# A decoder layer in which cross attention is one accumulating product of probabilities with context values already multiplied by the output weights

## The reference

```python
x = _layernorm(x + _L0_attn_ref(x, w_qkv, b_qkv, w_proj, b_proj))    # causal self attention, 16 heads of 16
x = _layernorm(x + _L0_xattn_ref(x, ctx, ctx, w_q, w_k, w_v, w_o))   # 16 heads of 64, 77 keys
x = _layernorm(x + _L0_ffn_ref(x, k0, k1, k2, s0, s1, s2))           # 256 -> 1024 -> 1024 -> 256, weights +1 / -1

def _L0_xattn_ref(query, key, value, w_q, w_k, w_v, w_o):
    q = (query @ w_q).reshape(B, Q, HEADS, HEAD_DIM).transpose(0, 2, 1, 3)
    k = (key @ w_k).reshape(B, Kl, HEADS, HEAD_DIM).transpose(0, 2, 1, 3)
    v = (value @ w_v).reshape(B, Kl, HEADS, HEAD_DIM).transpose(0, 2, 1, 3)
    scores = jnp.einsum('bhqd,bhkd->bhqk', q, k) * scale
    attn = jax.nn.softmax(scores, axis=-1)
    out = jnp.einsum('bhqk,bhkd->bhqd', attn, v)
    out = out.transpose(0, 2, 1, 3).reshape(B, Q, HEADS * HEAD_DIM)
    return out @ w_o
```

## Time and profile before

| what | value |
|---|---|
| time of three runs | 2335.62 us median (2334.43 to 2338.11) |
| the profiled execution: its own time | 2333.06 us |
| its span, first to last instruction | 2331.3 us |
| busy share of the span | PE 96%, PEld 79%, DVE 64%, ACT 42%, POOL 21% |
| first phase, from PE's first transpose to the last keys | 13.2 to 139.2 us |
| mean granted clock of TensorE | 0.987 |
| bytes moved by DMA | 135.85 MB |

### The profile page before, as it was taken

One profiled execution on the slowest core, in us unless ns is written; L12 is line 12 of the kernel. 1 busy time (PEld: TensorE's weight loads), 2 busy tenths in 40 slices (PEclk: granted clock), 3 DMA queues, 4 the chain that ended last, 5 costly groups with the idle time before them and its releaser, 6 DMA issues.

```text
span 2331.3 us, 52778 instructions
## 1 busy us (share of the span) xinstructions
PE 2233.6 (96%) x18516; PEld 1847.7 (79%) x18516; DVE 1485.0 (64%) x4685; ACT 970.2 (42%) x1797; POOL 482.0 (21%) x751
## 2 busy tenths in 40 slices
PE   7967899999999999999999999999999999999997
PEld 6856787888888888788888888888888888888876
DVE  3435666667667666667676666676676666676763
ACT  3313444444444444444444444444444444444432
POOL 2001212222222122212222222222221222122220
PEclk9978999999999999999999999999999999999999
DMA  6753332132333331233333322323333212233300
GB/s 209 228 115 53 54 58 45 39 50 37 56 56 56 56 50 41 42 44 49 56 56 56 56 42 39 47 41 56 56 56 56 48 40 44 40 53 56 56 25 10
DMA packets 150504, 135.85 MB, mean 58 GB/s; under 512 B 47746, under 2 KB 141986, under 8 KB 150402
## 3 DMA queue, kind: packets, MB, share of 16 engines
q1 hardware_dynamic: 150468, 135.37, 31.3%
HBM read 39.10 MB, written 28.59 MB: 29 GB/s over the span
## 4 chain that ended last, share of the span: by engine, by line
PE 81%; DVE 10%; issue 4%; ACT 3%; DMA 2%; POOL 1%; SPq 0%; DVEq 0%; POOLq 0%
PE ps L1028 10%; PE ps L1029 9%; PE ps L1169 9%; PE ps L988 8%; PE ps L1155 6%; PE ps L1011 5%; PE ps L1141 4%; PE ps L1082 4%; PE ps L1069 4%; PE ps L997 4%; DVE max L736 3%; PE ps L1039 3%; PE ps L1040 2%; PE ps L970 2%; PE ps L977 2%
## 5 line engine op out<-in xcount | busy, mean ns | idle before, releaser
L1028 PE MATMUL ps<-r_h,w 128*128 128x256 f16 x2048 | 464.4, 274 | 1.9 <-DVE r_l L682 1.9
L1029 PE MATMUL ps<-r_l,w 128*128 128x256 f16 x2048 | 462.1, 273 | 0.0
L471 ACT ACTIVATE r_h<-ps 128x512 f16<-128x512 f32 x256 | 152.6, 596 | 524.1 <-PE ps L1029 516.4
L697 DVE CUSTOM_DVE_ANT_0 junk<-ps,causal 128x128 bf16<-128x128 f32 (+1 forms) x1024 | 316.2, 353 | 60.1 <-PE ps L1058 53.8
L419 POOL TENSOR_TENSOR p<-p,inv 128x308 f32<-128x308 f32 x256 | 179.0, 699 | 479.5 <-DVE inv L753 479.5
L682 DVE SCALAR_TENSOR_TENSOR r_l<-ps,r_h 128x512 f16<-128x512 f32 x256 | 176.1, 688 | 119.5 <-ACT r_h L471 119.5
L524 ACT ACTIVATE probs<-ps 128x768 f32<-128x768 f32 x256 | 206.9, 809 | 106.9 <-PE ps L1069 106.8
L412 POOL TENSOR_SCALAR_AFFINE_SELECT probs<-probs 128x512 f32<-128x512 f32 x256 | 163.3, 638 | 393.8 <-ACT probs L524 393.7
L1028 PEld LDWEIGHTS ps<-r_h,w 128*128 128x128 f16 x2048 | 200.1, 98 | 49.6 <-issue 23.5
L1029 PEld LDWEIGHTS ps<-r_l,w 128*128 128x128 f16 x2048 | 200.9, 98 | 20.7
L758 DVE TENSOR_TENSOR o_l<-ps,o_h 128x512 fp32r<-128x512 f32 x128 | 88.5, 691 | 191.0 <-ACT o_h L516 190.6
(11 more groups left out here) (140 smaller groups left out, 4729.3 us busy)
## 6 DMA issues: line engine op xcount, KB each, us to landing
q_st<-o_h SPq DMA_DIRECT2D x192, 128.0 KB
k_bd<-o_h SPq DMA_DIRECT2D x192, 128.0 KB, 6.7
q<-q SPq DMA_DIRECT2D x128, 128.0 KB, 2.1
v_scratch<-v_out SPq DMA_DIRECT2D x44, 224.0 KB, 2.3
k_bd<-k_scratch SPq DMA_DIRECT2D x64, 154.0 KB
v<-v_scratch SPq DMA_DIRECT2D x32, 308.0 KB
x_in<-in_x SPq DMA_DIRECT2D x32, 256.0 KB, 4.6
out<-y SPq DMA_DIRECT2D x32, 256.0 KB, 2.2
```

The costliest lines, as they stand in the source:

```text
L697: dve.tensor_tensor_reduce(out=junk[:, e, b * P:b * P + width], in0=ps[:, bank + b, e * width:(e + 1) * width], in1=causal[:, (1 - b) * P: ...
L1028: pe.matmul(dst, w1[:, kk, m * P:(m + 1) * P], r0_h[:, kk, :], start=kk == 0, stop=False)
L1029: last = pe.matmul(dst, w1[:, kk, m * P:(m + 1) * P], r0_l[:, kk, :], start=False, stop=kk == KF - 1)
```

## The change

The values of a head are multiplied with that head's rows of `w_o` already in the first phase: per group and pair `context_values` makes the values transposed (heads' dimension on the partitions), ACT and DVE split them (`values_high`, `values_low`), `value_outputs` multiplies each half of 64 partitions with the 64 rows of `w_o` of its head, and the result, 256 numbers for each token and head, goes to `vo_scratch` (two halves of eight heads). In the loop a batch's 2 x 616 rows (77 tokens times 8 heads) are loaded (`load_value_outputs`), split by ACT and POOL, and used as the moving operand of `cross_output`: one product that accumulates over all token and head rows in ten tiles of 128 or 104 rows. The probabilities are laid out with eight heads innermost (`p2[P, 2, 2, 77, 8]`), transposed in those ten tiles, and split in high and low parts by ACT and DVE. `cross_values` and `cross_projection` are gone. Pieces of layer 1, self scores and self maxima are put at other places, the bank of the self scores is 2 for all pairs but 3 and 5, and self maxima 6 and 7 are made at the start of the next turn of the loop.

```diff
-            pe.wait_ge(const_pool, N_CONST)
+            pe.wait_ge(const_pool, 2)
...
+            def context_values(g, m):
...
+                for c, (w, a) in enumerate(((wv_h, ct_h), (wv_l, ct_h), (wv_h, ct_l))):
                     for kk in range(KD):
-                        last = pe.matmul(ps[0:CT, 4 + m % 2, :], a[g % 2][:, kk, rows], w[:, kk, cols],
+                        last = pe.matmul(ps[:, 3, 0:n], w[:, kk, m * P:(m + 1) * P], a[g % 2][:, kk, 0:n],
                                          start=c == 0 and kk == 0, stop=c == 2 and kk == KD - 1)
                 last.then_inc(pe_v2, 1)
+
+            def value_outputs(g, m):
...
+                for c, read in enumerate((a_vp, d_vp)):
...
+                    for a in range(2 * c, min(2 * c + 2, GROUPS[g])):
+                        for n, (v2t, w) in enumerate(((v2t_h, wo_h), (v2t_h, wo_l), (v2t_l, wo_h))):
+                            for e in range(2):
+                                half = slice(64 * e, 64 * e + 64)
+                                last = pe.matmul(ps[0:CT, 4 + 2 * c + e, (a % 2) * D:(a % 2 + 1) * D],
+                                                 v2t[k % 2][half, a * CT:(a + 1) * CT], w[half, m, :],
+                                                 start=n == 0, stop=n == 2)
+                    last.then_inc(pe_vp, 1)
...
+            def scores_by_query(i, n, after_cross=True):
+
                 if n == 1:
                     pe.wait_ge(d_mx, nth(i, 2 * H, 4))
+                if n == 3 and after_cross:
+                    pe.wait_ge(d_y2, nth(i, 1, 0))
...
                 if n >= 4:
-                    pe.wait_ge(d_mx, nth(i, 2 * H, 4 * (n - 1)))
-                bank = 0 if n < 2 else 2 + 4 * (n % 2)
+                    pe.wait_ge(d_mx, nth(i, 2 * H, 4 * n if n == 7 else 4 * (n - 1)))
+                bank = self_bank(n)
...
+            def cross_transposes(i, g, c, more=True):
+
+                unit = 3 * g + c
+                if c == 0:
+                    pe.wait_ge(g_p2, nth(i, KX, 4 * g + 4))
+                if unit == 0 and more:
+                    pe.wait_ge(d_mx, nth(i + 1, 2 * H, 8))
+                if unit >= 2:
+                    pe.wait_ge(a_p2t, nth(i, 6, unit - 1))
+                    pe.wait_ge(d_p2t, nth(i, 6, unit - 1))
+                for n in P2T_UNITS[c]:
+                    rows = tile_rows(n)
                     for b in range(TB):
...
+            def cross_output(i, g, c):
+
+                if c == 0:
+                    pe.wait_ge(g_vo, nth(i, 3, 2 + g))
+                    if g == 0:
+                        pe.wait_ge(a_q2, nth(i, 4, 4))
+                pe.wait_ge(a_p2t, nth(i, 6, 3 * g + c + 1))
+                pe.wait_ge(d_p2t, nth(i, 6, 3 * g + c + 1))
+                for n in P2T_UNITS[c]:
+                    rows, at = tile_rows(n), tile_at(g, n)
+                    for k, (p, w) in enumerate(((p2t_h, vo_h), (p2t_h, vo_l), (p2t_l, vo_h))):
+                        for b in range(TB):
+                            last = pe.matmul(ps[:, 6 + b, 0:D], p[0:rows, at, b * P:(b + 1) * P], w[0:rows, at, :],
+                                             start=g == 0 and n == 0 and k == 0, stop=g == 1 and n == VT - 1 and k == 2)
...
+                if more:
+                    scores_by_query(i + 1, 1)
                 cross_scores(i, 5)
-                cross_transposes(i, 1)
+                layer1_until(f, 16, 18)
                 cross_scores(i, 6)
...
+                layer1_until(f, 18, 20)
                 cross_scores(i, 7)
...
+                cross_transposes(i, 0, 0, more)
+                cross_transposes(i, 0, 1)
+                layer1_until(f, 20, 22)
+                cross_output(i, 0, 0)
+                cross_transposes(i, 0, 2)
+                cross_output(i, 0, 1)
+                cross_output(i, 0, 2)
+                layer1_until(f, 22, 24)
+                cross_transposes(i, 1, 0)
+                cross_transposes(i, 1, 1)
+                layer1_until(f, 24, 26)
+                cross_output(i, 1, 0)
+                cross_transposes(i, 1, 2)
+                cross_output(i, 1, 1)
+                cross_output(i, 1, 2)
                 if more:
                     scores_by_query(i + 1, 2)
...
+                layer1_until(f, 26, 27)
                 if more:
                     scores_by_query(i + 1, 3)
...
+        p2 = sb("p2", [P, TB, 2, SK, HG], F32)
...
+        def unit_probs(t):
+
+            h = 2 * (t % 4)
+            return p2[:, :, t // 4, :, h:h + 2].rearrange("p b k e -> p b e k")
```

More of the change, by code:

```diff
@@ L114, in decoder_layer @@
         xt_l = sb("xt_l", [P, KD, S], F32R)
-        o2_h = sb("o2_h", [P, KX, S], F32R)
-        o2_l = sb("o2_l", [P, KX, S], F32R)
+        p2t = sb("p2t", [P, 2, 2 * VT, S], F32R)
+        p2t_h = p2t[:, 0]
+        p2t_l = p2t[:, 1]
+        qk_h = p2t[:, 0, 0:2 * KD, :]
+        qk_l = p2t[:, 0, 2 * KD:4 * KD, :]
+        vo_h = sb("vo_h", [P, 2 * VT, D], F32R)
+        with ExitStack() as loaded:
+            vo = loaded.enter_context(nc.sbuf_tensor("vo", [P, 2 * VT, D], F32))
+        vo_l = sb("vo_l", [P, 2 * VT, D], F32R)
         probs = sb("probs", [P, 6, 512], F32)
@@ L142, in decoder_layer @@
         ps = stack.enter_context(nc.psum_tensor("ps", [P, 8, 512], F32))
-        w_in = [sem(f"w_in{n}") for n in range(5)]
+        w_in = [[sem(f"w_in{n}_{c}") for c in range(2)] for n in range(3)] + [sem(f"w_in{n}") for n in (3, 4)]
         kb_in = [sem(f"kb_in{n}") for n in range(2)]
@@ new lines, in save_value_outputs @@
+            def save_value_outputs(g, j):
+                k = KX * g + j
+                for c, ready in enumerate((a_vp, d_vp)):
+                    tiles = min(2, GROUPS[g] - 2 * c)
+                    row = (TILE0[g] + 2 * c) * CT
+                    sp.wait_ge(ready, k + 1)
+                    sp.dma_start(vo_d[j // 4, row:row + tiles * CT, (j % 4) * 512:(j % 4 + 1) * 512]
+                                 .rearrange("(a p) f -> p a f", p=CT), vo_out[k % 2][:, 2 * c:2 * c + tiles, :])\
+                      .then_inc(vo_saved[k % 2][c], 16)
@@ new lines, in _ @@
+            load_ctx(0)
+            for c in range(2):
+                for n, w in enumerate((w_v, w_k)):
+                    sp.dma_start(first_part(CONTEXT_WEIGHTS[n][0], c),
+                                 first_part(w.rearrange("(k p) n -> p k n", p=P), c)).then_inc(w_in[n][c], 16)
+                rows = slice(0, 2 * P) if c == 0 else slice(2 * P, KX * P)
+                sp.dma_start(first_part(wo, c), w_o[rows, :].rearrange("(k p) n -> p k n", p=P))\
+                  .then_inc(w_in[2][c], 16)
@@ L307, in load_keys_values, with load_value_outputs @@
                     sp.dma_start(k2_bd[64 * e:64 * e + 64, :, e * SK:(e + 1) * SK],
-                                 k2_d[:, 64 * e:64 * e + 64, rows].rearrange("m p t -> p m t")).then_inc(ctx_loaded, 16)
-                sp.dma_start(v2[:], v2_d[rows, :]).then_inc(ctx_loaded, 16)
+                                 k2_d[:, 64 * e:64 * e + 64, rows].rearrange("m p t -> p m t")).then_inc(k2_loaded, 16)
+            def load_value_outputs(i):
+                for g in range(2):
+                    full = vo_rows[g][bass.ds(i * GROUP_ROWS, (VT - 1) * P), :]
+                    part = vo_rows[g][bass.ds(i * GROUP_ROWS + (VT - 1) * P, LAST_ROWS), :]
+                    n0, n1 = tile_at(g, 0), tile_at(g, VT - 1)
+                    sp.dma_start(vo[:, n0:n0 + VT - 1, :], full.rearrange("(n p) d -> p n d", p=P))\
+                      .then_inc(vo_loaded, 16)
+                    sp.dma_start(vo[0:LAST_ROWS, n1, :], part).then_inc(vo_loaded, 16)
             def load(j):
@@ L536, in attention @@
             def attention(i, first, f, first_f=False, more=True):
-                self_probs(i, 0)
+                for n in range(4):
+                    self_probs(i, n)
                 negated_max(i, 1)
-                for n in range(1, 5):
-                    self_probs(i, n)
+                self_probs(i, 4)
                 if not first:
@@ L563, in attention @@
                 self_output_high(i, 1)
+                for n in range(3):
+                    value_outputs_high(i, n)
                 if not first:
@@ L816, in attention @@
                     cross_sum(i, t - 1)
+                    if t == 4 and more:
+                        self_max(i + 1, 1)
+                    if t == KX - 2:
+                        cross_probs_low(i, 0, 0)
                 cross_inverse(i, KX - 2)
+                cross_probs_low(i, 0, 1)
                 cross_sum(i, KX - 1)
-                cross_output_low(i, 0)
                 cross_inverse(i, KX - 1)
-                if more:
-                    self_max(i + 1, 1)
-                cross_output_low(i, 1)
-                cross_output_low(i, 2)
-                cross_output_low(i, 3)
+                cross_probs_low(i, 0, 2)
+                for c in range(3):
+                    cross_probs_low(i, 1, c)
```

(5 more changed lines are left out.)

493 lines of the change are left out of this document (263 added, 230 removed).

## The result

The changed kernel takes 2864.53 us (median of 4 runs, 2861.97 to 2867.43) against 2335.02 us (2333.85 to 2338.11): 1.2266 times as long, 95% interval 1.2244 to 1.2287. It is slower, as forecast, but by 529.5 us and not by 145; 2864.5 lies far outside the range of 2380 to 2560.

What follows compares the result with a forecast made beforehand. TensorE, 96% busy, was taken as the bound at 66.1 us a batch. Profiled 2333.1 + 66 (first phase) - 5 (earlier start) + 3 (first scores and batch) + 81 (loop) = 2478, plus 2.5 to the median: about 2480 us, range 2380 to 2560.

Steps and rivals of the forecast that it cites:

- The first phase: Making keys, values and new products: +66 us, -5 for earlier PE start, +3 for first scores and batch; ends near 200.
- theory 1: Experiments' theory: POOL's subtraction holds up DVE's apply and TensorE, the larger part; strided softmax and sequential walk the rest.
- Strided probabilities: Cross softmax with eight heads innermost: slower reads in sum and exponential, nothing on writes or POOL; +1.3 us a batch.
- What ends last in the batch afterwards: Loop's chain from first scores to last product walked in sequence: spared PE time becomes waiting, batch 1.3 us longer.
- What PE is spared: Cross part's transposes and products: 5.1 us less PE work a batch, 163 us in all, if nothing else ends later.
- The rivals of that step: Slower first phase: row halves one after the other (+52 us) or DMAs bind (+35), 2515 to 2560 us; chance 0.25.
- The rival "faster": PE stays fed in the loop, chain hidden: 5.1 us less a batch, 2236 us; chance 0.12.

Runs made afterwards that it cites:

- Run 1: Kernel before the change plus three POOL subtractions on unneeded data, behind the deviation of x1: 2565.93 us, ratio 1.0984.
- run 4: Changed kernel with the residual sum of x1 kept in PSUM for DVE's apply, POOL's subtraction left in place: 2632.42 us, ratio 1.127.
- run 2: Changed kernel with the split of loaded products moved ahead: POOL subtracts before the deviation of x1, ScalarE copies earlier: 2674.65 us, ratio 1.1444.
- run 8: Changed kernel with head-then-key order, 12 loads a batch, first transposes after two pairs, split's subtractions in three DVE idle times: 2482.83 us, ratio 1.0658.
- runs 5: Changed kernel with probabilities and product rows ordered head then key, loaded with 24 transfers a batch instead of 4: 3017.77 us, ratio 1.2915.
- run 6: Changed kernel, split's subtraction in one DVE idle time, head-then-key order, 12 loads a batch, maxima's transfers ahead of keys': 2593.91 us, ratio 1.1104.

## Why the prediction was wrong

**The step that failed** is the last one of "The first phase": "ScalarE's split of the loaded products … and POOL's … lie before the cross part, where both wait", costed at nothing. POOL does wait there, but its 5.9 us block DVE's apply beside it. Run 1 prices that step by itself at 229 us, run 4 at 232 us, and run 2 shows 190 us of it saved by place alone. At 43% of the 529.5 us it is the largest single part, though not the larger part of the loss that theory 1 made it. I asked who waits for POOL's result, and not what its instruction holds up on DVE while it runs. (The 6.4 us recorded for it are a slip: 2560 elements at 699 ns for 308 are 5.8, and 5.9 were measured.) The x1 part, for which I had forecast no change, is 7.0 of the 10.8 us by which the batch shown (79.5 us) is longer than forecast (66.1 + 2.6); the self part is 3.1 of them, the cross part 0.7.

The same pairing stands a second time in the batch, and no run takes it out: POOL's sum of the next input and the bias, an old instruction, now meets the apply of x2, whose two pieces take 1.49 us instead of 0.73, since fewer self maxima stand ahead of it on DVE.

```profile
989.01 1.49 DVE L797 TENSOR_SCALAR x<-x,mv,rstd 128x256 f32<-128x256 f32 x2
...
988.76 1.27 POOL L468 TENSOR_TENSOR xb<-x_in,bias_p 128x512 f32<-128x512 f32 x1
```

It is so in run 8 too, and not before nor in run 1. What these 0.76 us of DVE cost the self part is not shown.

**"Strided probabilities"** had the right mechanism and sizes for two of five instructions: sum 464 to 707 ns (forecast +0.22 us), exponential 458 to 788 (forecast +0.3). "Nothing on the writes and on POOL" was wrong: the subtraction of the maximum, which writes with the step, went from 479 to 735, and POOL's normalisation from 699 to 886. The maximum, which touches no strided tensor, stayed at 469. On the path it is 2.4 us a batch in the cross part, by runs 5 and 6 alike (2.7 for the whole batch in run 6, queue order included), where I had 1.3 and a bound of 1.9. The Trainium skill's rule of the 16-byte line (SBUF — State Buffer, Door 1: The DMA port swizzle) speaks of every access, and the trace agrees with it on reads and writes of all three engines.

**"What ends last in the batch afterwards"** was right for the cross part: I had the sum of x2 26.7 + 1.3 = 28.0 us behind the first maximum, measured 28.7, before 24.5. In part that is luck: with contiguous accesses the cross part is 25.9 to 26.0 us, 0.7 under my 26.7, and the strides cost 2.4 where I had 1.3, so two errors cancel. It was wrong for the self part, from that sum to the sum of x1: 32.4 us before; forecast (6.5 for the scores by key where it was 8.6, then 1.25 later) some 0.9 less, measured 34.6. In that stretch TensorE waits, on the mean of all batches, 1.9 us for the residual sum, 1.9 for the maxima's transfers, 1.3 for row maxima and 1.0 for the low part of transposed x2. The places were those that I named, save the last; the first scores by key start 7.4 us behind the sum (at 990.99), not 6.5.

**"What PE is spared"**: the cross part has 23.67 us of busy TensorE where it had 23.96, in more time, and the self part 29.49 instead of 32.17, since fewer pieces of layer 1 are left for it. The work went down and none of it reached the time. The forecast of 5.1 us a batch isn't confirmed: run 8, with its waits mostly gone, has 62.35 us busy where 65.32 were, 3.0 less, with one stretch at a clock of 0.95.

**"The first phase"**: the two products of a pair do go side by side. Six of them follow each other at 0.11 to 0.12 us for two in the timeline of the first phase, and the last starts at 219.3 us, where keys and values ended at 139 and I had said near 200:

```profile
216.12 0.28 PE L1129 MATMUL ps<-wo_l,v2t_h 64*112 64x256 f32 x2
216.24 0.28 PE L1129 MATMUL ps<-wo_h,v2t_l 64*112 64x256 f32 x2
```

The group with the longest waits in that phase, and the window that answers to the first of the earlier trace rows:

```profile
L1112 PE MATMUL ps<-ct_h,wv_h 128*128 128x448 f32 (+1 forms) x96 | 27.9, 373 | 12.0 <-DVE v2t_l L771 9.8 <-DVE ct_l L761 2.2
```

```profile
60.00:110.00 50.00, 48.95 (x412) 41.62 (x411) 24.45 (x25) 26.66 (x36) 0.00 (x0) 0.98 0.91 294
```

The rivals of that step are both out: halves one after the other would have given over 240 us, and the DMA, at a share of 0.91, did not stop TensorE, which is busy 98% of the window. Of the 20 us that I was short, 12 are waits for DVE. The granted clock is 0.90 from 17 to 60 us, behind the first of these waits, and 0.97 over the whole phase, where it was 1.00 before; 0.03 of 220 us is some 6 us more, an estimate that no run tests. (The rounds are 48, 32 with 24 of the new products and 16 with 18, and not 44 with 24; at 0.25 us each that adds 1 us.) Up to the first sum of x2 it is 100.3 us instead of the 67 that my terms make with one batch's 2.6; 6.1 of it are the blocked apply of the first batch (in run 2 the first sum is at 334.9 instead of 341.0), 20 the first phase; the other 7 stay open.

**The rival "faster"** had its point of decision at 3.1 us of new waiting a batch. TensorE's busy time in the batch fell by 1.1 us and the batch grew by 13.4: 14.5 us of new idle time. Even the best version (62.35 us busy in 68.2) has 5 us more than before.

## What to carry to other kernels

An engine that is free is not free of charge: before work is moved to POOL, look at what DVE does in the same stretch, and keep long POOL instructions away from DVE's SBUF-to-SBUF instructions on the path, or let these read PSUM. Work spared on an engine that is 96% busy becomes waiting if the same edit joins steps that used to overlap, and a wait can cost more than its length when the clock falls behind it (5.3 us of waiting made the x1 part 7.3 us longer in run 1). Count every transfer that a queue has to issue ahead of a small urgent one: a better layout lost more in SP's queue than it won on three engines.

## What the runs showed of the hardware

- Beside POOL's subtractions of 1024 and 512 elements, DVE's layer-norm apply of 256 elements takes up to 3.6 us instead of 0.41 (its line: shortest, median and longest, x1 and x2 together). One piece can stay blocked over two POOL instructions that follow each other. The one that starts first is not held up: in run 2 a product that started 0.03 us ahead of POOL kept its 0.42, and POOL took 2.63 to 2.65 us for its 2.34. Behind POOL's start, a product of two SBUF tensors goes from 0.42 to 1.47, a difference of two up to 3.91; a reciprocal (1.75) and instructions with an input in PSUM (0.68, 0.54) are not held up.

```profile
L797 DVE TENSOR_SCALAR x<-x,mv,rstd x128: 400/1886/3646, 297.3 to 2825.8; 128x256 f32<-128x256 f32 x128
```

- Four bytes at a step of 32 cost, for 308 elements: DVE +0.24 us reading, +0.26 writing, ScalarE +0.33 for both, POOL +0.19 for both.
- Products that contract over 64 rows each, one in either half of the partitions, run two at a time in 0.11 to 0.12 us for 256 columns.
- SP needs 0.47 us on average for each of the 24 loads of at most 77 rows (11.31 us for all).
